# Tail of a fused vision-transformer kernel: weights' parts transposed first, result summed in other banks, one-bank router, fewer filler matmuls, second output transfer issued by ScalarE

## The chip, the cores and the metric

The program runs on one core of a Trainium2 chip. The metric is the device time of one execution in microseconds (us), the median of three executions. The profile shows one further execution. Engines are called PE (TensorE), DVE (VectorE), ACT (ScalarE), POOL (GpSimd) and SP (SyncE), as in the profile.

## What is computed

The reference runs two transformer layers on 8 images of 64 tokens with 64 features: patch embedding and position, attention, a gated feed-forward, a second attention and last a mixture of 8 experts. Only the last part is touched by the change:

```python
def _moe(tokens, router_w, w1, b1, w2, b2):
    logits = tokens @ router_w.T
    probs = softmax(logits)
    rw, re = top_k(probs, 2)
    rw = rw / rw.sum(-1, keepdims=True)
    combine = zeros((N, 8)).at[arange(N)[:, None], re].set(rw)
    out = tokens
    for e in range(8):
        h = gelu(tokens @ w1[e] + b1[e])
        y = h @ w2[e] + b2[e]
        out = out + combine[:, e:e + 1] * y
    return out
...
h = h + _L1_ffn_ref(_layernorm(h), ...)
```

The result adds `h` (the tokens after the second attention), the normalised tokens and the weighted experts.

## The kernel before, in words

512 tokens are kept as two halves of 256: the tile `xC[3]` holds the normalised tokens, features on partitions, with half c=0 on partitions 0 to 63 and half c=1 on 64 to 127. Four slots of 128 tokens are numbered s = 2c + j. Each engine has a program written out by hand, in its own block, and runs it in order; engines meet at semaphores (`wait_ge`, `then_inc`). PSUM has eight banks, `B[0]` to `B[7]`. All float32 matmuls other than transposes are run in two passes, so the trace counts two instructions for each; a transpose by `tr` counts one. `keep_clock(bank, n)` (line 683, instructions at line 687) issues n matmuls of zeros, 128x512 in bfloat16, into a bank that nobody needs at that time; they are called fillers below. Line numbers here are those of the kernel before.

The tail, after the layer norm of the second attention's result:

- PE: the router, four matmuls of 64 rows each, slots of half 0 into `B[2]` and of half 1 into `B[3]` (lines 984 to 988); the first expert layer, eight matmuls for four pairs q of experts, into `B[4]` to `B[7]` (989 to 994); three fillers; after the first two gelus have read `B[4]` and `B[5]` (`s_eg` 2) and after POOL's sum `resT3` (`s_res3`), the opening products of the result `Y = (B[4], B[5])`: the residual by an identity and `Wo1` on `ctxT` (1000 to 1004); two fillers; four transposes of the float32 weights `comb` (1007), four of `comb3`, the same weights as three bfloat16 parts (1012); two fillers; four matmuls with `sel3` that spread the weights of pair q over the hidden rows (1021); three fillers; the products with `b2e` (1026); the second expert layer (1032), which sums all four pairs into `Y`.
- DVE: reads the logits (632), ranks them and forms `lgd`, waits for ACT's tanh `lgt`, forms `comb` and `comb3` (651 to 657), copies the transposed parts to `comb3T` (659), multiplies the gelus by the spread weights, `gs` (668, the last pair in two pieces, one for each j), adds a bias to the second half of the result (670) and copies its transpose to `h4` (672).
- ACT: the gelus `ge` of pairs 0 and 1, the tanh, the gelus of pairs 2 and 3 (426 to 435), a copy `combT` (437), the first half of the result (439) and of its transpose (441).
- SP issues both output transfers (264 and 266), each after its half of `h4` is written.
- POOL has in its queue, in this order: the scaling `WoS` of the first attention's output weights (298), the gather `attr` of edge attributes (309, waits for `s_edge`), two constants, and near the end `resT3` (326).

```python
            for q in range(4):
                for j in range(2):
                    pe.wait_ge(s_gs, q + 1 if q < 3 else 4 + j)
                    for c in range(2):
                        ins = mm(Y[j][rows[c], 0:P], lhsT=w2e[:, q, :], rhs=gs[:, q, c * HALF + j * P:c * HALF + (j + 1) * P], ...
```

Of the kernel before, what the change touches and what calls it, by code (L numbers as in the profile page):

```python
# [6 lines left out]
P = 128  # L7
# [3 lines left out]
D = 64  # L11
# [30 lines left out]
def vit_tower(nc, I, packs, out):  # L42
# [25 lines left out]
    with ctx:  # L68
# [97 lines left out]
        lg = sb("lg", [P, SLOTS, EXPERTS])  # L166
        lgd = sb("lgd", [P, SLOTS, EXPERTS])
# [62 lines left out]
        s_bar = sem("bar_ready")  # L230
# [4 lines left out]
        C3 = B[3][0:3 * EXPERTS, 0:NT // 2].bitcast(bf16)  # L235

# [10 lines left out]
        def _(sp):  # L247
# [22 lines left out]
        def _(pool):  # L270
# [36 lines left out]

            pool.wait_ge(s_edge, 1)
# [20 lines left out]
        def _(act):  # L329
# [96 lines left out]
            for q in range(4):  # L426
                if q == 2:
# [9 lines left out]
            sc.activation(combT[:, :], B[1][0:EXPERTS, :], ACT.Copy).then_inc(s_ct_ev, 1)  # L437
            act.wait_ge(s_fin, 1)
            sc.activation(yT[:, 0, :], B[4][:, 0:P], ACT.Identity, bias=bo_col[:, 0:1]).then_inc(s_yT_a, 1)
            act.wait_ge(s_yR, 1)  # L440
            sc.activation(h4[:, :, :].rearrange("p (c s) d -> p s c d", c=2)[:, 0, :, :],
                          B[6][:, 0:P].rearrange("p (c d) -> p c d", c=2), ACT.Copy).then_inc(s_out_a, 1)

        @block.vector
        def _(dve):
# [186 lines left out]
            link(ve.tensor_copy(lg[:, :, :].rearrange("p (c j) e -> p c (j e)", c=2), psum[:, 2:4, 0:2 * EXPERTS]))  # L632
# [27 lines left out]
            for q in range(4):  # L660
# [4 lines left out]
                         for tile in (gs[:, q, :], ge[:, q, :], (B[2], B[0], B[1], B[3])[q])]  # L665
                for js in (slice(0, 2),) if q < 3 else (slice(0, 1), slice(1, 2)):
# [3 lines left out]
            ve.tensor_scalar(yT[:, 1, :], B[5][:, 0:P], bo_col[:, 0:1], None, ALU.add).then_inc(s_yT_v, 1)  # L670
            dve.wait_ge(s_yR, 2)
            ve.tensor_copy(h4[:, :, :].rearrange("p (c s) d -> p s c d", c=2)[:, 1, :, :],
                           B[7][:, 0:P].rearrange("p (c d) -> p c d", c=2)).then_inc(s_out_v, 1)

        @block.tensor
        def _(pe):
# [330 lines left out]
            for s in range(SLOTS):  # L1007
                ins = tr(B[1][0:EXPERTS, s * P:(s + 1) * P], comb[:, s, :], P)
# [137 lines left out]
```

## Time and profile before

| | us |
|---|---|
| median of three executions | 74.75 (74.56 to 74.87) |
| profiled execution, its own time | 74.51 |
| its span in the profile | 72.7 |
| PE busy in the span | 64.6 (89%) |
| DVE busy | 41.9 (58%) |
| ACT busy | 29.2 (40%) |
| fillers (line 687), all 63 | 19.9 |
| mean granted TensorE clock | 0.992 |

The span runs from the first to the last event of the core; the execution's time contains 1.8 us more around it. A matmul that is pipelined behind another is counted from its own start, so busy times of neighbours overlap: the distance between two starts tells what a matmul takes of PE's time. "PEld" is the weight load that belongs to a matmul. "PEclk" or granted clock is 1.00 at 2.4 GHz and 0.50 at 1.2 GHz.

### The profile page before, as it was taken

The numbers are of one execution on the slowest core, as the hardware profiler recorded it, in microseconds if no ns is written. First come the engines' busy times: TensorE is split into PE (matmuls) and PEld (weight loads), VectorE is DVE, ScalarE is ACT, GpSimd is POOL, SyncE is SP. The second block draws the span as 40 slices with busy tenths as digits, with TensorE's granted clock in tenths as the row PEclk, the third lists the DMA queues.
The fourth block names the chain that finished last, engine by engine and source line by source line (L and its number), as shares of the span: only waits on it lengthen the run. The fifth ranks groups of instructions, "written<-read, shape, count | busy, mean of one in ns | idle before, by whom it ended". The sixth has DMA issues, their size and how long they took to land.

```text
span 72.7 us, 1994 instructions
## 1 busy us (share of the span) xinstructions
PE 64.6 (89%) x843; PEld 39.5 (54%) x843; DVE 41.9 (58%) x108; ACT 29.2 (40%) x63; POOL 13.0 (18%) x29
## 2 busy tenths in 40 slices
PE   3995996999999999989979969799999889999930
PEld 1330554777887585445435645577954285543910
DVE  2590199484799983536642397997540157429430
ACT  0330104404497821296925060488023748530030
POOL 6800094000004920538030000000000030000000
PEclk9999999999999999999999999999999999999996
DMA  0799999900000000000000000000000000000003
GB/s 5 180 394 390 373 224 263 265 16 0 0 9 0 0 9 0 0 0 5 0 0 0 0 0 9 0 9 0 0 9 5 0 0 0 0 0 0 0 0 72
DMA packets 2389, 4.07 MB, mean 56 GB/s; under 512 B 779, under 2 KB 1229, under 8 KB 2381
## 3 DMA queue, kind: packets, MB, share of 16 engines
q1 hardware_dynamic: 1840, 3.55, 16.8%
q10 hardware_dynamic: 509, 0.40, 1.7%
q8 instruction: 6, 0.10, 0.6%
q14 instruction: 2, 0.02, 0.1%
q0 software_dynamic: 32, 0.00, 0.1%
HBM read 3.82 MB, written 0.13 MB: 54 GB/s over the span
## 4 chain that ended last, share of the span: by engine, by line
PE 64%; DVE 13%; DMA 9%; ACT 4%; POOL 3%; issue 3%; DVEq 0%; ACTq 0%; POOLq 0%
PE psum L687 10%; DMA Xt<-in_x_dram 9%; PE psum L681 6%; DVE top L503 3%; POOL WoS L298 3%; PE psum L697 3%; PE psum L893 3%; PE psum L939 3%; PE psum L789 3%; PE psum L740 3%; PE psum L991 3%; PE psum L1032 2%; PE psum L716 2%; DVE E L601 2%; DVE top L599 2%
## 5 line engine op out<-in xcount | busy, mean ns | idle before, releaser
L687 PE MATMUL psum<-warm 128*128 128x512 bf16 x63 | 19.9, 429 | 1.2 <-DVE warm L455 1.2
L687 PEld LDWEIGHTS psum<-warm 128*128 128x128 bf16 x63 | 5.8, 107 | 8.1 <-issue 4.3
L298 POOL TENSOR_TENSOR WoS<-pack_attn,top 128x256 f32<-128x256 f32 x5 | 3.1, 647 | 11.1 <-DVE top L510 11.1
L468 DVE TENSOR_TENSOR onehot<-idb,iota 128x2048 bf16<-128x2048 bf16 x4 | 4.8, 1244 | 0.0
L326 POOL TENSOR_TENSOR resT<-hT,xC 128x256 f32<-128x256 f32 x1 | 0.7, 724 | 20.5 <-DVE xC L630 20.5
L405 ACT ACTIVATE E<-E 128x512 f32<-128x512 f32 x4 | 2.5, 630 | 3.2 <-DVE E L601 3.1
L348 ACT ACTIVATE lv<-psum,eps 128x256 f32<-128x256 f32 x4 | 1.9, 473 | 3.5 <-PE psum L729 0.9
L599 DVE TENSOR_REDUCE top<-psum 128x8 f32<-128x512 f32 x4 | 2.7, 686 | 0.4 <-PE psum L908 0.4
L434 ACT ACTIVATE ge<-psum,pack_moe 128x512 f32<-128x512 f32 x4 | 2.5, 679 | 1.1 <-PE psum L991 1.1
L908 PE MATMUL psum<-kT,qT 9*64 9x64 f32 x128 | 2.1, 231 | 0.9 <-DVE qT L587 0.7
L773 PE MATMUL psum<-top,pack_ident 128*128 128x256 f32 x12 | 2.9, 387 | 0.0
L668 DVE TENSOR_TENSOR gs<-ge,psum 128x512 f32<-128x512 f32 (+1 forms) x5 | 2.5, 577 | 0.5 <-PE psum L1021 0.5
L697 PE MATMUL psum<-Xt,pack_wp 128*64 128x256 f32 x16 | 2.2, 390 | 0.8 <-DMA Xt<-in_x_dram 0.8
L601 DVE TENSOR_TENSOR E<-psum,top 128x512 f32<-128x512 f32 x4 | 2.8, 692 | 0.1
L503 DVE TENSOR_REDUCE top<-psum 128x8 f32<-128x512 f32 x4 | 2.6, 684 | 0.4 <-PE psum L765 0.4
L789 PE MATMUL psum<-WoS,E 128*64 128x64 f32 x64 | 2.7, 227 | 0.1
L630 DVE SCALAR_TENSOR_TENSOR xC<-psum,bo_col,rs 128x256 f32<-128x256 f32 x1 | 0.5, 484 | 4.0 <-ACT rs L350 4.0
L789 PEld LDWEIGHTS psum<-WoS,E 128*64 128x64 f32 x64 | 2.2, 137 | 0.9 <-ACT E L376 0.5
L345 ACT ACTIVATE sq<-psum 128x256 f32<-128x256 f32 x3 | 1.1, 383 | 4.0 <-PE psum L831 1.7
L908 PEld LDWEIGHTS psum<-kT,qT 9*64 9x64 f32 x128 | 1.7, 130 | 1.9 <-ACT qT L400 1.0
L508 DVE TENSOR_REDUCE top<-E 128x8 f32<-128x512 f32 x4 | 2.6, 648 | 0.0
L681 PE MATMUL psum<-pack_ident,E 128*128 128x128 f32 x16 | 2.5, 278 | 0.1
(200 smaller groups left out, 131.7 us busy)
## 6 DMA issues: line engine op xcount, KB each, us to landing
Xt<-in_x_dram SPq DMA_DIRECT2D x1, 1024.0 KB, 6.4
Xt<-in_x_dram SPq DMA_DIRECT2D x1, 512.0 KB, 7.5
pack_both<-in_both_dram SPq DMA_DIRECT2D x2, 240.2 KB, 8.8
pack_moe<-in_moe_dram SPq DMA_DIRECT2D x1, 450.0 KB, 9.8
pack_mid<-in_mid_dram SPq DMA_DIRECT2D x1, 327.5 KB, 10.0
pack_attn<-in_attn_dram SPq DMA_DIRECT2D x1, 288.0 KB, 8.1
pack_expert<-in_expert_dram SPq DMA_DIRECT2D x2, 130.0 KB, 9.3
pack_wp<-in_wp_dram ACTq DMA_DIRECT2D x1, 192.0 KB, 6.0
```

Source lines behind the costliest of these rows:

```text
L298: gp.tensor_tensor(WoS[:, s, 4 * u:4 * u + 4, :].rearrange("p (b n) d -> p b n d", b=2), bc(WoT[:, 2 * u:2 * u + 2, :], 1, 2), bc(top0[:, ...
L468: ve.tensor_tensor(onehot[:, 16 * k:16 * k + 16, :], bc(idb[:, k, :], 1, 16), iota16[:, :, :], ALU.is_equal).then_inc(s_hot, 1)
L503: ve.tensor_reduce(top0[:, 0, s, :].rearrange("p (m q) -> p m q", m=2), S, X, ALU.max, negate=True).then_inc(s_mx0, 1)
L508: ve.tensor_reduce(top0[:, 1, s, :], E0[:, s, :, :], X, ALU.add).then_inc(s_sum0, 1)
L599: ve.tensor_reduce(top, S, X, ALU.max).then_inc(s_mx1, 1)
L601: ve.tensor_tensor(E1[:, s, :, :].rearrange("p (q g) t -> p q g t", g=2), S, bc(top, 3, TOK), ALU.subtract).then_inc(s_sub1, 1)
L681: return nc.tensor.transpose(o, i, ident[0:n, 0:n])
L687: mm(B[bank][:, :], lhsT=warm[:, 0:P], rhs=warm[:, :], start=True, stop=True)
L697: mm(B[0][rows[c], 0:HALF], lhsT=Wp[:, q, :], rhs=Xt[:, c, q, :], start=(q == 0), stop=False)
L773: ins = mm(B[2 * s + m][:, 0:HALF], lhsT=ident, rhs=bc(top0[:, 0, s, 4 * m:4 * m + 4], 2, TOK), start=False, stop=True, skip_group_check=True)
L789: ins = mm(B[2 * s][rows[b], 0:D], lhsT=E0[:, s, i, :], rhs=WoS[:, s, i, :], start=(q == 0), stop=(q == 3))
L908: ins = mm(B[4 * c + hh][b * D:(b + 1) * D, col:col + TOK], lhsT=qT1[rows_, g, tok:tok + TOK], rhs=kT1[rows_, g, tok:tok + TOK], start=Tru ...
```

## The change

It changes seven things in the tail.

1. Router: a new tile `rwB`, [128, 16], holds the router's weights twice, as a block diagonal, zeros elsewhere. POOL fills it (a memset and two copies of 64x8), placed in its queue after `WoS` and ahead of the gather; it waits there for the load of the experts' weights. The router is then two matmuls over all 128 rows, both into `B[2]`, in place of four over 64 rows, and DVE reads the logits from that bank alone.
2. `Y` becomes `(B[0], B[1])`. Its opening products wait only for `s_res3` and follow the first expert layer at once.
3. Fillers: ten in this stretch (3, 2, 2, 3) become one, between the opening products and the transposes.
4. The transposes of `comb3` come first, those of `comb` (now into `B[2]`) behind them; PE waits once, for `s_comb` 5.
5. The spread weights of pair q go to `B[4 + q]`, the banks of the experts' hidden values, so PE waits for gelus 0 and 1 ahead of pair 0, and for gelus 2 and 3 ahead of pair 2. The wait for `combT` moves from ahead of pair 2 to ahead of the `b2e` products.
6. The result's halves are transposed into `B[2]` and `B[3]`.
7. ACT, not SP, issues the transfer of the second half, after waiting for DVE's `s_out_v`.

```diff
+            pool.wait_ge(in_expert, 32)
+            gp.memset(rwB[:, :], 0.0).then_inc(s_rwb, 1)
+            pool.wait_ge(s_rwb, 1)
+            for c in range(2):
+                half = slice(c * D, (c + 1) * D)
+                gp.tensor_copy(rwB[half, c * EXPERTS:(c + 1) * EXPERTS], rwT[half, :]).then_inc(s_rwb, 1)
+            pool.wait_ge(s_rwb, 3)
             pool.wait_ge(s_edge, 1)
...
+            act.wait_ge(s_out_v, 1)
+            act.dma_start(out_v[1], h4_v[:, 1, :, :]).then_inc(out_done, 16)
...
-            pe.wait_ge(in_expert, 32)
+            pe.wait_ge(s_rwb, 3)
             pe.wait_ge(s_x, 4)
-            for s in range(SLOTS):
-                c, j = s // 2, s % 2
-                ins = mm(B[2 + c][:, j * EXPERTS:(j + 1) * EXPERTS], lhsT=xC[3][rows[c], j * P:(j + 1) * P], rhs=rwT[rows[c], :],
+            for j in range(2):
+                ins = mm(B[2][:, 2 * j * EXPERTS:2 * (j + 1) * EXPERTS], lhsT=xC[3][:, j * P:(j + 1) * P], rhs=rwB[:, :],
                          start=True, stop=True)
...
-            Y = (B[4], B[5])
+            Y = (B[0], B[1])
             blocks = [slice(j * P, (j + 1) * P) for j in range(2)]
-            keep_clock(0, 3)
-            pe.wait_ge(s_eg, 2)
+
             pe.wait_ge(s_res3, 1)
...
-            keep_clock(0, 2)
-            pe.wait_ge(s_comb, 1)
-            for s in range(SLOTS):
-                ins = tr(B[1][0:EXPERTS, s * P:(s + 1) * P], comb[:, s, :], P)
-            ins.then_inc(s_ct, 1)
+            keep_clock(3, 1)
+
             pe.wait_ge(s_comb, 5)
             pe.wait_ge(const_moe, 2)
-            for s in range(SLOTS):
-                ins = nc.tensor.transpose(C3[:, s * P:(s + 1) * P], comb3[:, s, :, :], ident_h[:, :])
+            for j in range(2):
+                for c in range(2):
+                    ins = nc.tensor.transpose(C3[:, c * HALF + j * P:c * HALF + (j + 1) * P], comb3[:, 2 * j + c, :, :], ident_h[:, :])
             ins.then_inc(s_c3, 1)
-            keep_clock(2, 2)
+            for j in range(2):
+                for c in range(2):
+                    ins = tr(B[2][0:EXPERTS, c * HALF + j * P:c * HALF + (j + 1) * P], comb[:, 2 * j + c, :], P)
+            ins.then_inc(s_ct, 1)
             pe.wait_ge(s_c3_ev, 1)
             for q in range(4):
 
-                if q == 2:
-                    pe.wait_ge(s_ct_ev, 1)
-                mm((B[2], B[0], B[1], B[3])[q][:, :], lhsT=sel3[:, q, :], rhs=comb3T[:, :], start=True, stop=True).then_inc(s_cr, 1)
-            pe.wait_ge(s_eg, 4)
-            keep_clock(6, 3)
+                if q % 2 == 0:
+                    pe.wait_ge(s_eg, q + 2)
+                mm(B[4 + q][:, :], lhsT=sel3[:, q, :], rhs=comb3T[:, :], start=True, stop=True).then_inc(s_cr, 1)
+            pe.wait_ge(s_ct_ev, 1)
```

How it moves instructions. In these rows a name is the tile written, then `<-` and the tiles read; `warm` is the fillers' operand, `sel` is `sel3`, `comb` with 24x128 is `comb3`.

PE's program from behind the first expert layer to the first spread weights, before:

```order
L687 MATMUL psum<-warm 128x512 x3
L1001 MATMUL psum<-resT,pack_ident 128x128 [waits residual3_ready,expert_gelu]
L1003 MATMUL psum<-ctxT,pack_mid 64x128 x2
L1001 MATMUL psum<-resT,pack_ident 128x128
L1003 MATMUL psum<-ctxT,pack_mid 64x128 x2
L687 MATMUL psum<-warm 128x512 x2
L681 MATMUL psum<-pack_ident,comb 8x128 [waits comb_ready]
L681 MATMUL psum<-pack_ident,comb 8x128 x3
L1013 MATMUL psum<-ident_h,comb 24x128 [waits const_moe,comb_ready]
L1013 MATMUL psum<-ident_h,comb 24x128 x3
L687 MATMUL psum<-warm 128x512 x2
L1021 MATMUL psum<-comb3T,sel 128x512 [waits comb3T_ready]
```

The same place in the changed program, where lines 1006 and 1008 are the opening products, 1016 the transposes of `comb3` and 687 those of `comb`:

```order
L1006 MATMUL psum<-resT,pack_ident 128x128 [waits residual3_ready]
L1008 MATMUL psum<-ctxT,pack_mid 64x128 x2
L1006 MATMUL psum<-resT,pack_ident 128x128
L1008 MATMUL psum<-ctxT,pack_mid 64x128 x2
L693 MATMUL psum<-warm 128x512
L1016 MATMUL psum<-ident_h,comb 24x128 [waits const_moe,comb_ready]
L1016 MATMUL psum<-ident_h,comb 24x128 x3
L687 MATMUL psum<-pack_ident,comb 8x128 x4
L1027 MATMUL psum<-comb3T,sel 128x512 [waits expert_gelu,comb3T_ready]
```

Seven fillers became one, the transposes of the parts stand ahead of those of `comb`, and the opening products no longer wait for a gelu.

PE's program from the second spread weights to the second expert layer, before:

```order
L1021 MATMUL psum<-comb3T,sel 128x512
L1021 MATMUL psum<-comb3T,sel 128x512 [waits combT_ready]
L1021 MATMUL psum<-comb3T,sel 128x512
L687 MATMUL psum<-warm 128x512 [waits expert_gelu]
L687 MATMUL psum<-warm 128x512 x2
L1026 MATMUL psum<-combT,pack_moe 64x128 x4
L1032 MATMUL psum<-gs,pack_moe 64x128 [waits expert_scaled]
```

The same place in the changed program:

```order
L1027 MATMUL psum<-comb3T,sel 128x512
L1027 MATMUL psum<-comb3T,sel 128x512 [waits expert_gelu]
L1027 MATMUL psum<-comb3T,sel 128x512
L1031 MATMUL psum<-combT,pack_moe 64x128 [waits combT_ready]
L1031 MATMUL psum<-combT,pack_moe 64x128 x3
L1037 MATMUL psum<-gs,pack_moe 64x128 [waits expert_scaled]
```

The three fillers are gone and the wait for `combT` stands behind all four matmuls.

POOL's program from the scaling of the first attention's weights, before:

```order
L298 TENSOR_TENSOR WoS<-pack_attn,top 128x256 [waits rinv_ready,const_l1]
L298 TENSOR_TENSOR WoS<-pack_attn,top 128x256
L298 TENSOR_TENSOR WoS<-pack_attn,top 128x256 [waits rinv_ready] x3
L309 DMA attr<-in_L_attn_edge_attr_dram,edge_u 64x3 [waits edge_ready]
L312 TENSOR_SCALAR gate_bar<-pack_mid 128x64 [waits in_mid]
```

and in the changed program:

```order
L297 TENSOR_TENSOR WoS<-pack_attn,top 128x256 [waits rinv_ready,const_l1]
L297 TENSOR_TENSOR WoS<-pack_attn,top 128x256
L297 TENSOR_TENSOR WoS<-pack_attn,top 128x256 [waits rinv_ready] x3
L308 MEMSET rwB 128x16 [waits in_expert]
L312 COPY rwB<-pack_expert 64x8 [waits router_ready]
L312 COPY rwB<-pack_expert 64x8
L315 DMA attr<-in_L_attn_edge_attr_dram,edge_u 64x3 [waits edge_ready,router_ready]
L318 TENSOR_SCALAR gate_bar<-pack_mid 128x64 [waits in_mid]
```

Three small instructions stand between the scaling and the gather.

## Rows read from the trace of the kernel before

**Rows 1.** By stretch: length, busy PE, PEld, DVE, ACT, POOL, granted clock, DMA share, GB/s.
```profile
15.96:23.35 7.39, 7.36 (x161) 6.20 (x162) 5.80 (x12) 4.62 (x13) 0.47 (x1) 1.00 0.01 2
49.84:53.37 3.53, 3.53 (x77) 3.08 (x75) 2.13 (x7) 1.09 (x2) 0.00 (x0) 1.00 0.02 5
```

**Rows 2.** Timeline of PE in the tail: start us, us, engine, line, operation, count.
```profile
58.50 0.62 PE L986 MATMUL psum<-pack_expert,xC 64*128 64x8 f32 x8 [0.70 <-DVE xC L630]
58.94 2.01 PE L991 MATMUL psum<-xC,pack_expert 64*128 64x256 f32 x16
...
60.89 0.82 PE L687 MATMUL psum<-warm 128*128 128x512 bf16 x3
61.54 0.45 PE L1001 MATMUL psum<-resT,pack_ident 128*128 128x128 f32 x2
61.92 0.44 PE L1003 MATMUL psum<-ctxT,pack_mid 64*64 64x128 f32 x4
...
63.08 0.60 PE L687 MATMUL psum<-warm 128*128 128x512 bf16 x2
63.52 0.60 PE L681 MATMUL psum<-pack_ident,comb 128*8 128x128 f32 x4
64.05 0.39 PE L1013 MATMUL psum<-ident_h,comb 128*24 128x128 bf16 x4
64.38 0.61 PE L687 MATMUL psum<-warm 128*128 128x512 bf16 x2
64.95 1.03 PE L1021 MATMUL psum<-comb3T,sel 24*128 24x512 bf16 x4
65.91 0.82 PE L687 MATMUL psum<-warm 128*128 128x512 bf16 x3
66.66 0.65 PE L1026 MATMUL psum<-combT,pack_moe 8*64 8x128 f32 x8
67.25 1.97 PE L1032 MATMUL psum<-gs,pack_moe 128*64 128x128 f32 x32
```

**Rows 3.** Timeline of ACT and DVE in the tail.
```profile
61.57 1.25 ACT L434 ACTIVATE ge<-psum,pack_moe 128x512 f32<-128x512 f32 x2
62.43 0.19 DVE L657 TENSOR_TENSOR comb<-part,comb 128x32 bf16<-128x32 f32 x1
64.16 0.59 ACT L437 ACTIVATE combT<-psum 8x512 f32<-8x512 f32 x1 [1.33 <-PE psum L681]
64.48 0.41 DVE L659 COPY comb3T<-psum 24x512 bf16<-24x512 bf16 x1 [1.86 <-PE psum L1013]
65.44 2.55 DVE L668 TENSOR_TENSOR gs<-ge,psum 128x512 f32<-128x512 f32 x5 [0.55 <-PE psum L1021]
```

**Rows 4.** Timeline: DVE's last copy and the issue of its transfer.
```profile
70.03 0.29 DVE L672 COPY h<-psum 128x128 f32<-128x128 f32 x1 [0.42 <-PE psum L681]
...
70.58 0.47 SPq L266 DMA_DIRECT2D out_dram<-h  x1
```

**Rows 5.** Timeline: full-row float32 weights elsewhere, early fillers, an early issue by ACT.
```profile
1.17 5.30 PE L687 MATMUL psum<-warm 128*128 128x512 bf16 x12 [1.17 <-DVE warm L455]
1.61 0.93 ACTq L333 DMA_DIRECT2D pack_pos<-in_pos_dram  x1
47.10 0.66 PE L681 MATMUL psum<-pack_ident,E 128*128 128x128 f32 x4
47.59 0.59 PE L687 MATMUL psum<-warm 128*128 128x512 bf16 x2
```

**Rows 6.** POOL's timeline, and the page's DMA traffic (GB/s) in 40 slices.
```profile
23.45 2.51 POOL L298 TENSOR_TENSOR WoS<-pack_attn,top 128x256 f32<-128x256 f32 x4
29.83 1.08 POOL L309 DMA_INDIRECT attr<-in_L_attn_edge_attr_dram,edge_u  x1 [3.87 <-DVEq L542]
...
58.44 0.72 POOL L326 TENSOR_TENSOR resT<-hT,xC 128x256 f32<-128x256 f32 x1 [20.53 <-DVE xC L630]
...
GB/s 5 180 394 390 373 224 263 265 16 0 0 9 0 0 9 0 0 0 5 0 0 0 0 0 9 0 9 0 0 9 5 0 0 0 0 0 0 0 0 72
```

More of the change, by code:

```diff
@@ L166, in vit_tower @@
         lg = sb("lg", [P, SLOTS, EXPERTS])
+        rwB = sb("rwB", [P, 2 * EXPERTS])
         lgd = sb("lgd", [P, SLOTS, EXPERTS])
@@ L235, in vit_tower @@
         C3 = B[3][0:3 * EXPERTS, 0:NT // 2].bitcast(bf16)
+        out_v = out.rearrange("(c s b) t d -> s (b t) c d", c=2, s=2)
+        h4_v = h4[:, :, :].rearrange("p (c s) d -> p s c d", c=2)
         block = ctx.enter_context(nc.Block())
@@ L436, in _ @@
             act.wait_ge(s_ct, 1)
-            sc.activation(combT[:, :], B[1][0:EXPERTS, :], ACT.Copy).then_inc(s_ct_ev, 1)
+            sc.activation(combT[:, :], B[2][0:EXPERTS, :], ACT.Copy).then_inc(s_ct_ev, 1)
             act.wait_ge(s_fin, 1)
-            sc.activation(yT[:, 0, :], B[4][:, 0:P], ACT.Identity, bias=bo_col[:, 0:1]).then_inc(s_yT_a, 1)
+            sc.activation(yT[:, 0, :], B[0][:, 0:P], ACT.Identity, bias=bo_col[:, 0:1]).then_inc(s_yT_a, 1)
             act.wait_ge(s_yR, 1)
-            sc.activation(h4[:, :, :].rearrange("p (c s) d -> p s c d", c=2)[:, 0, :, :],
-                          B[6][:, 0:P].rearrange("p (c d) -> p c d", c=2), ACT.Copy).then_inc(s_out_a, 1)
+            sc.activation(h4_v[:, 0, :, :], B[2][:, 0:P].rearrange("p (c d) -> p c d", c=2), ACT.Copy).then_inc(s_out_a, 1)
+            act.wait_ge(s_out_v, 1)
+            act.dma_start(out_v[1], h4_v[:, 1, :, :]).then_inc(out_done, 16)
         @block.vector
@@ L631, in _ @@
             dve.wait_ge(s_lg, 1)
-            link(ve.tensor_copy(lg[:, :, :].rearrange("p (c j) e -> p c (j e)", c=2), psum[:, 2:4, 0:2 * EXPERTS]))
+            link(ve.tensor_copy(lg[:, :, :].rearrange("p s e -> p (s e)"), B[2][:, 0:SLOTS * EXPERTS]))
             dve.wait_ge(in_moe, 16)
@@ L664, in _ @@
                 parts = [tile.rearrange("p (c s t) -> p c s t", c=2, s=2)
-                         for tile in (gs[:, q, :], ge[:, q, :], (B[2], B[0], B[1], B[3])[q])]
+                         for tile in (gs[:, q, :], ge[:, q, :], B[4 + q])]
                 for js in (slice(0, 2),) if q < 3 else (slice(0, 1), slice(1, 2)):
@@ L669, in _ @@
             dve.wait_ge(s_fin, 2)
-            ve.tensor_scalar(yT[:, 1, :], B[5][:, 0:P], bo_col[:, 0:1], None, ALU.add).then_inc(s_yT_v, 1)
+            ve.tensor_scalar(yT[:, 1, :], B[1][:, 0:P], bo_col[:, 0:1], None, ALU.add).then_inc(s_yT_v, 1)
             dve.wait_ge(s_yR, 2)
-            ve.tensor_copy(h4[:, :, :].rearrange("p (c s) d -> p s c d", c=2)[:, 1, :, :],
-                           B[7][:, 0:P].rearrange("p (c d) -> p c d", c=2)).then_inc(s_out_v, 1)
+            ve.tensor_copy(h4_v[:, 1, :, :], B[3][:, 0:P].rearrange("p (c d) -> p c d", c=2)).then_inc(s_out_v, 1)
         @block.tensor
@@ L1036, in _ @@
             pe.wait_ge(s_yT_a, 1)
-            tr(B[6][:, 0:P], yT[:, 0, :], P).then_inc(s_yR, 1)
+            tr(B[2][:, 0:P], yT[:, 0, :], P).then_inc(s_yR, 1)
             pe.wait_ge(s_yT_v, 1)
-            tr(B[7][:, 0:P], yT[:, 1, :], P).then_inc(s_yR, 1)
+            tr(B[3][:, 0:P], yT[:, 1, :], P).then_inc(s_yR, 1)
 _OUTS = [((8, 64, 64), 'float32')]
```

7 lines of the change are left out of this document (2 added, 5 removed).

## The prediction

> **What bounds the kernel now.** I read the chain of waits first: from 58.50 us on it is PE alone, with no wait for another engine, until the last sum; after that ACT, PE and DVE take turns and the transfer ends the span. So I read PE's timeline of the tail next [rows 2] and asked of each group whether PE was doing needed work or bridging a wait. It bridges: ten of its matmuls are fillers, at 60.89 (3), 63.08 (2), 64.38 (2) and 65.91 (3). Then I read DVE and ACT beside it [rows 3]. The last part of the weights is ready at 62.43 + 0.19 = 62.62, yet DVE waits 1.86 us for PE's transposes, because PE is at its opening products, two fillers and the transposes of `comb` first. DVE's products `gs` end at 65.44 + 2.55 = 67.99, and PE goes on to sum for another 1.2 us. PE's program order bounds the tail, fillers included. Last I read the end of the span [rows 4] and the granted clock by stretch [rows 1].
>
> **The change, part by part.** I take distances between starts, since they are what a matmul takes of PE. Everything counts from 58.50, when `xC[3]` is ready; nothing before it moves (POOL's new work is costed last).
>
> Router. Before: eight passes, 58.50 to 58.94, 0.44 [rows 2]. Now four passes over all 128 rows with 16 columns moving. No row of before shows that form. Nearest are float32 weights of 128x128: the opening product takes (61.92 − 61.54)/2 = 0.19 a pass with 128 columns moving [rows 2], the transposes (47.59 − 47.10)/4 = 0.12 [rows 5]. So four passes lie between 4 × 0.055 = 0.22, the pace of the old form (a gain of 0.22), and 4 × 0.19 = 0.76 (a loss of 0.32). I take 0.13 each, 0.52, since with few columns moving the load is what remains and the transposes' row is the nearest to that: a **loss of 0.08**. It delays the logits and the first expert layer alike, hence the weights and the gelus too.
> The Trainium skill speaks otherwise here (TensorE: Matmul & The Clock Gate, section LDWEIGHTS): a load's time goes by its columns, not its rows, so half as many loads of 128 columns would cost half. By that the router would gain 0.22 and the sum below would be 0.30 larger. The two rows above, 0.055 a pass over 64 rows and 0.12 to 0.19 over 128, speak against it.
>
> First expert layer: 58.94 to 60.89, 1.95, unchanged; it now ends at 60.97.
>
> Opening products: 61.54 to 63.08, 1.54, unchanged. The three fillers ahead (0.65) go, and with other banks the wait for gelus 0 and 1 goes too. `resT3`, which they do wait for, is ready at 58.44 + 0.72 = 59.16 [rows 6]. They end at 60.97 + 1.54 = 62.51, and the one filler that remains ((61.54 − 60.89)/3 = 0.22) at 62.73.
>
> Transposes. They need the last part of the weights, 62.62 + 0.08 = 62.70, so PE waits next to nothing; I start them at 62.75. The four of `comb3` take 64.38 − 64.05 = 0.33 and DVE's copy began 0.43 after the first of them [rows 2, 3]: it runs from 63.18 to 63.59. The four of `comb` take 0.53 and now lie beside that copy, ending at 63.61.
>
> Spread weights: from 63.65 (0.06 after the copy, as before), 0.96 long. The gelus they wait for end about 61.53 and at 61.57 + 1.25 + 0.08 = 62.90 [rows 3], both earlier. The new place of the wait for `combT` costs nothing: ACT's 0.59 starts at about 63.65, ends at 64.25, and PE asks for it at 64.61. That cover is 0.36; without it `b2e` would slip by what is missing.
>
> `b2e` from 64.61, 0.59 long; second expert layer from 65.20, before 67.25 [rows 2]. That is **2.05 earlier**, and by parts: fillers 0.65 + 0.22 (one of the two at 63.08) + 0.57 + 0.75 = 2.19, less 0.08 router, less about 0.06 of now exposed waits.
>
> Does DVE hold it up? The first `gs` begins 0.49 after the spread weights, at 64.14, and the five end 2.55 later at 66.69. PE, unhindered, would end its 32 passes 1.97 + 65.20 = 67.2; the last four need DVE's last piece and would take until about 66.69 + 0.4 = 67.1. PE still ends last, by 0.1: the two are nearly level, so this part can gain no more from PE alone.
>
> End of the span: everything behind the last sum comes 2.05 earlier, by the same steps. Before, DVE's copy ended at 70.03 + 0.29 = 70.32, but SP issued the second transfer at 70.58, because it was still issuing the first [rows 4]. ACT is idle, so it issues some 0.05 after the copy: 0.21 gained. Against that, an issue by ACT took 0.93 early in the program, beside SP's issues, where SP's took 0.47 here [rows 4, 5]. So the ends are a gain of 0.3 and a loss of 0.25; I take **0.20 gained**, since here only two transfers are in flight.
>
> POOL: three small instructions between `WoS`, done at 25.96, and the gather at 29.83, for which POOL idles 3.87 [rows 6]. Even at the 0.63 of a `WoS` product each they fit with 1.9 to spare: 0. The experts' weights have long landed: traffic ends in the ninth of 40 slices of 1.82 us, by 16.4 us [rows 6].
>
> Sum: 2.05 + 0.20 = 2.25. The profiled execution took 74.51, so it would take 72.26; the median of the three is 0.24 above it, so I predict 74.75 − 2.25 = **72.5 us**. A difference under 0.5% (0.37 us) is about what a measurement of this kernel cannot tell from none.
>
> **The rivals.**
>
> A. *The clock falls (slower).* After the one filler at 62.5 PE has none to the end, with eight transposes, small matmuls and waits. If it dropped to 1.2 GHz, every pass would take up to twice as long. A price at such a pace is in the trace: the twelve fillers at the start are (5.30 − 0.43)/11 = 0.44 apart, against 0.22 in the tail [rows 5, 2] (the granted-clock column says 1.00 there too, so I use the row for its size alone). From the spread weights on, 0.96 + 0.59 + 1.97 + 0.38 (the two last transposes at 0.19) = 3.90 would be added: 72.5 + 3.9 = 76.4. It decides from 2.25 us of added PE time, so only when the clock falls by about the start of the second expert layer; a fall behind that leaves the change faster. For it: ten fillers stood where one will. Against it: two stretches without a filler, 7.4 us of small matmuls and 3.5 us with eight transposes and tiny products among them, both at 1.00 [rows 1], and PE here has no gap over 0.1 us until the last sum. I give it 9%: 7% slower, 2% near no change.
> The Trainium skill has a rule for this rival (TensorE: Matmul & The Clock Gate, part 4): transposes do not count as busy for the clock in the same way. By it the clock would be nearer to falling in the stretch of eight transposes; the row from 49.84 to 53.37, with as many, shows no such thing.
>
> B. *The logits' chain takes over.* PE reaches the transposes with 0.03 us in hand, so whatever delays DVE's or ACT's chain shows at once: with the router at its dear end, 0.32 lost in place of 0.08, both chains shift and the gain is 2.0; if in addition DVE's `gs` runs slower against PE, now that both end together, 0.3 more is lost: 74.75 − 1.7 = 73.05. For it: DVE and PE nearly level. Against: nothing they share is used more than before. 12%.
>
> C. *ACT's issue is as dear as the dear row*, or the two transfers land no sooner side by side: 2.05 − 0.25 = 1.8 gained, 72.95. 10%.
>
> D. *The router costs half*, and ACT issues at 0.38: 2.25 + 0.30 + 0.1 = 2.65, 72.1. 12%.
>
> The forecast itself, 2.0 to 2.5 gained, has 57%.
>
> **How the numbers follow.** The forecast and B, C, D (91%) are faster by 1.7 to 2.65, and span 72.1 to 73.05. Adding 0.3 for the executions' own spread and for two bounds falling together on either side gives a range of 71.8 to 73.4; left out are rival A and the corners. Of A's 9%, 7 are slower and 2 within 0.5%; another 1% within 0.5% is kept for losses that I don't see. So: faster 0.90, same 0.03, slower 0.07.
>
> **What the profile after would show.** Four router passes about 0.13 apart. No filler behind the first expert layer; opening products from about 61.0; `comb3T` at 63.2 and DVE's wait ahead of it under 1 us in place of 1.86. `gs` from 64.1. Second expert layer ending near 67.2, and its four last passes close behind DVE's last piece. An output issue on ACT at some 68.3, overlapping SP's. The gather still at 29.8 and a granted clock of 1.00 to the last transpose. I am wrong if the clock column falls ahead of 67 us, if PE shows waits of over 0.2 us for DVE at the transposes, or if the first expert layer starts later than 59.2.

## The result, and the profile after

| | before | after |
|---|---|---|
| median, us | 74.66 | 72.52 |
| lowest to highest of four, us | 74.56 to 74.87 | 72.24 to 72.68 |
| profiled execution: time, span, us | 74.51, 72.7 | 72.43, 70.6 |
| PE busy, us | 64.6 | 62.7 |
| fillers, all of the program | 63, 19.9 us | 54, 17.4 us |

The ratio is 0.9705, with an interval of 0.9665 to 0.9745: **2.1 us faster**, where 72.5 us was predicted (71.8 to 73.4). In some executions of most kernels here TensorE's granted clock falls for a while; the ratios, and the times where not all are listed, are of executions in which it did not.

One thing that the list of the change's parts left out: with the new router the logits come out as slot 2j + c in place of 2c + j, and the loops over `comb` and `comb3` are renumbered to match. It moves no instruction.

The first part of the changed kernel's page (busy us of each engine, share of the span, instructions):

```profile
PE 62.7 (89%) x830; PEld 38.7 (55%) x830; DVE 41.8 (59%) x108; ACT 29.2 (41%) x63; POOL 13.5 (19%) x32
```

PE's share of the span is 89% before and after. The share says nothing about the gain, since a filler counts as busy as a product does; that nine fillers are gone is seen in the last row of the table. The timeline of the tail shows the rest (the columns of [rows 2 to 4]):

```profile
58.57 0.59 PE L991 MATMUL psum<-rwB,xC 128*128 128x16 f32 x4 [0.70 <-DVE xC L637]
59.09 2.00 PE L997 MATMUL psum<-xC,pack_expert 64*128 64x256 f32 x16
59.20 0.19 DVE L639 COPY lg<-psum 128x32 f32<-128x32 f32 x1 [0.77 <-PE psum L991]
...
61.02 0.49 PE L1006 MATMUL psum<-resT,pack_ident 128*128 128x128 f32 x2
...
62.47 0.19 DVE L664 TENSOR_TENSOR comb<-part,comb 128x32 bf16<-128x32 f32 x1
...
62.59 0.39 PE L693 MATMUL psum<-warm 128*128 128x512 bf16 x1
...
62.91 0.39 PE L1016 MATMUL psum<-ident_h,comb 128*24 128x128 bf16 x4
...
63.34 0.41 DVE L666 COPY comb3T<-psum 24x512 bf16<-24x512 bf16 x1 [0.67 <-PE psum L1016]
...
63.81 1.03 PE L1027 MATMUL psum<-comb3T,sel 24*128 24x512 bf16 x4
63.87 0.59 ACT L443 ACTIVATE combT<-psum 8x512 f32<-8x512 f32 x1 [1.00 <-PE psum L687]
64.30 2.54 DVE L675 TENSOR_TENSOR gs<-ge,psum 128x512 f32<-128x512 f32 x5 [0.55 <-PE psum L1027]
...
64.77 0.65 PE L1031 MATMUL psum<-combT,pack_moe 8*64 8x128 f32 x8
...
65.35 1.98 PE L1037 MATMUL psum<-gs,pack_moe 128*64 128x128 f32 x32
67.16 0.37 ACT L445 ACTIVATE yT<-psum,bo_col 128x128 f32<-128x128 f32 x1 [2.70 <-PE psum L1037]
...
68.16 0.29 DVE L679 COPY h<-psum 128x128 f32<-128x128 f32 x1 [0.42 <-PE psum L687]
68.25 0.41 SPq L265 DMA_DIRECT2D out_dram<-h  x1
68.48 0.41 ACTq L449 DMA_DIRECT2D out_dram<-h  x1
```

The router starts at 58.57, so nothing ahead of it gained: all of the difference lies in the tail. I read it as distances from the router's first pass, since these don't shift when the start of the program does. They repeat well: to the second expert layer it is 6.78 in this profile and in that of `e_sp_issues`, whose tail has the same instructions up to there. To the second expert layer it is 67.25 − 58.50 = 8.75 before [rows 2] and 65.35 − 58.57 = 6.78 after, 1.97 less. To the issue of the second output it is 70.58 − 58.50 = 12.08 [rows 2, 4] and 68.48 − 58.57 = 9.91, 2.17 less. The span falls by 2.1 and not by 2.17, because the router starts 0.07 later. DVE's wait for the transposes of `comb3` is 0.67 in place of 1.86 [rows 3].

The granted clock in the stretch with the eight transposes (length, busy us of PE, PEld, DVE, ACT and POOL with their counts, clock, DMA share, GB/s):

```profile
62.00:64.00 2.00, 2.00 (x16) 0.97 (x16) 1.01 (x6) 1.00 (x3) 0.00 (x0) 1.00 0.00 0
```

It is full speed, 2.4 GHz, here and in every other stretch from 55 us to the last output's issue.

### The profile page after: what moved, and what is told of

It reads as the page before. It is cut to its first block, busy times and chain, and to the rows that moved or that the text cites. A ratio compares the mean times of both kernels' runs of the same rounds, so it can differ in the third digit from the quotient of the medians.

```text
span 70.6 us, 1972 instructions
## 1 busy us (share of the span) xinstructions
PE 62.7 (89%) x830; PEld 38.7 (55%) x830; DVE 41.8 (59%) x108; ACT 29.2 (41%) x63; POOL 13.5 (19%) x32
## 4 chain that ended last, share of the span: by engine, by line
PE 66%; DMA 9%; DVE 7%; ACT 6%; issue 3%; POOL 3%; DVEq 0%; ACTq 0%; POOLq 0%
DMA Xt<-in_x_dram 9%; PE psum L693 9%; PE psum L687 6%; POOL WoS L297 3%; PE psum L703 3%; PE psum L914 3%; PE psum L899 3%; PE psum L945 3%; PE psum L795 3%; PE psum L997 3%; PE psum L746 3%; ACT E L377 2%; PE psum L1037 2%; PE psum L722 2%; PE psum L859 2%
## 5 line engine op out<-in xcount | busy, mean ns | idle before, releaser
L693 PE MATMUL psum<-warm 128*128 128x512 bf16 x54 | 17.4, 437 | 1.2 <-DVE warm L462 1.2
L693 PEld LDWEIGHTS psum<-warm 128*128 128x128 bf16 x54 | 5.3, 108 | 7.0 <-issue 3.6
```

The lines of the kernel that those rows point to most:

```text
L693: mm(B[bank][:, :], lhsT=warm[:, 0:P], rhs=warm[:, :], start=True, stop=True)
```

## The experiments

The theory: PE's order bounded the tail, so each part is worth what it takes off PE's path, and the parts add up (fillers 0.65 + 0.22 + 0.57 + 0.75; order of transposes and banks to let them go; ACT's issue 0.20; router −0.08). The rivals: DVE's chain takes over when PE is freed; the clock needs the fillers; the gain comes from the banks or the issue and the fillers were free. Distances are from the router's first pass, and "to w2e" is to the second expert layer's first.

**Fillers alone, on the kernel before** (`e_before_nofill`).

```diff
-            keep_clock(0, 3)
             pe.wait_ge(s_eg, 2)
...
-            keep_clock(0, 2)
+            keep_clock(0, 1)
...
-            keep_clock(2, 2)
             pe.wait_ge(s_c3_ev, 1)
...
-            keep_clock(6, 3)
```

> The kernel before with nine of the ten fillers of the tail taken out and nothing else (the one left stands behind the opening products). Theory: the fillers are only part of the gain; the opening products still wait for the gelus 0 and 1 (until about 61.45 us), the float32 transposes still stand ahead of the parts', so the second expert layer starts near 66.2 instead of 67.25: about 1.0 us gained on before, 73.65 us. Rival: the fillers are all of it: 2.2 us gained, 72.5 us.

Measured: the one execution without a fall of the clock took 73.75, where before took 74.79 to 75.1 on that chip; three more, 74.93 to 75.59, had a lower mean clock, in the profiled one early in the program and not in the tail. The distances in that tail:

```profile
60.36 0.62 PE L986 MATMUL psum<-pack_expert,xC 64*128 64x8 f32 x8 [0.70 <-DVE xC L630]
...
63.36 0.49 PE L1000 MATMUL psum<-resT,pack_ident 128*128 128x128 f32 x2 [0.55 <-ACT ge L434]
...
65.69 0.39 PE L1012 MATMUL psum<-ident_h,comb 128*24 128x128 bf16 x4
...
66.59 1.03 PE L1019 MATMUL psum<-comb3T,sel 24*128 24x512 bf16 x4 [0.51 <-DVE comb3T L659]
...
68.14 1.99 PE L1029 MATMUL psum<-gs,pack_moe 128*64 128x128 f32 x32
```

To w2e 7.78, which is 0.97 less than before: not quite half of the change. The first three fillers give nothing, because PE then waits for gelus 0 and 1 in their place, as the bracket behind L1000 shows: to the opening products it is 3.00, against 61.54 − 58.50 = 3.04 before [rows 2]. Nor do the two at the spread weights: from the transposes of `comb3` to the spread weights it is 66.59 − 65.69 = 0.90, as before (64.95 − 64.05 [rows 2]), since PE waits for DVE's copy there (the bracket behind L1019). What comes back is one filler (about 0.2) and the three ahead of `b2e` (0.75). A filler is a cost only where no wait stands behind it that would last as long.

**The wait for the gelus, put back into the change** (`e2_wait_gelu`): what moving the sums to other banks is worth.

```diff
+            pe.wait_ge(s_eg, 2)
             pe.wait_ge(s_res3, 1)
```

> The changed kernel with the wait for gelus 0 and 1 put back ahead of the opening products (as if Y still lay in their banks). Theory: the products start at 61.65 instead of 61.02, and all behind is 0.6 us later: second expert layer 7.4 us after the router's first pass instead of 6.78, 73.1 us. Rival: the wait is hidden by that for the weights (62.7 us), under 0.1 us.

Measured: 73.00 in one execution. The opening products start 61.56 − 58.48 = 3.08 after the router instead of 2.45, and w2e 7.41 instead of 6.78: **0.63**.

```profile
58.48 0.59 PE L991 MATMUL psum<-rwB,xC 128*128 128x16 f32 x4 [0.70 <-DVE xC L637]
...
61.56 0.49 PE L1007 MATMUL psum<-resT,pack_ident 128*128 128x128 f32 x2 [0.56 <-ACT ge L440]
...
63.88 0.41 DVE L666 COPY comb3T<-psum 24x512 bf16<-24x512 bf16 x1 [1.30 <-PE psum L1017]
...
65.89 1.98 PE L1038 MATMUL psum<-gs,pack_moe 128*64 128x128 f32 x32
```

DVE's wait grows by the same 0.63, from 0.67 to 1.30. So the first three fillers and this wait are one cost of 0.65 that could only go together, and the other banks are what lets both go.

**The transposes in their old order** (`e_order_old`).

```diff
+            pe.wait_ge(s_comb, 1)
+            for j in range(2):
+                for c in range(2):
+                    ins = tr(B[2][0:EXPERTS, c * HALF + j * P:c * HALF + (j + 1) * P], comb[:, 2 * j + c, :], P)
+            ins.then_inc(s_ct, 1)
             pe.wait_ge(s_comb, 5)
...
-            for j in range(2):
-                for c in range(2):
-                    ins = tr(B[2][0:EXPERTS, c * HALF + j * P:c * HALF + (j + 1) * P], comb[:, 2 * j + c, :], P)
-            ins.then_inc(s_ct, 1)
```

> The changed kernel with the transposes of comb ahead of those of its parts, as before. Theory: the parts' transposes start 0.53 later, less what PE waited there: comb3T, the spread weights and everything behind 0.4 to 0.5 us later than in the changed kernel, 72.95 us. Rival: the order is worth nothing, since PE must do both anyway: 72.5 us.

Measured: 73.22 and 73.51, and 74.58 and 76.58 with a lower mean clock; the ratio of the first two to before, 0.9884 (0.976 to 1.0008), says little. In the profile, at full clock, it is to w2e 66.14 − 58.92 = 7.22, **0.44** more than the change.

```profile
58.92 0.59 PE L991 MATMUL psum<-rwB,xC 128*128 128x16 f32 x4 [0.70 <-DVE xC L637]
...
62.94 0.39 PE L693 MATMUL psum<-warm 128*128 128x512 bf16 x1
...
63.16 0.60 PE L687 MATMUL psum<-pack_ident,comb 128*8 128x128 f32 x4
63.69 0.39 PE L1021 MATMUL psum<-ident_h,comb 128*24 128x128 bf16 x4
...
66.14 1.99 PE L1038 MATMUL psum<-gs,pack_moe 128*64 128x128 f32 x32
```

It is the 0.53 of the four transposes of `comb`, less 0.10: the filler holds PE for 0.22 here (62.94 to 63.16) and for 0.32 in the change (62.59 to 62.91).

**Three fillers back, ahead of `b2e`** (`e_fill_back`). They had looked as if they bridged the wait for the gelus.

```diff
+            keep_clock(3, 3)
             pe.wait_ge(s_ct_ev, 1)
```

> The changed kernel with three fillers put back between the spread weights and the b2e products. Theory: PE, not DVE, ends the sum, by about 0.1 us, so three fillers of 0.22 cost 0.6 to 0.65 us: 73.15 us. Rival: DVE's products bound this part, PE has slack there and the fillers cost under 0.2 us.

Measured: 73.19, 73.01 and 73.66, ratio 0.9792 (0.9739 to 0.9845); a fourth took 76.37 at a mean clock of 0.954.

```profile
58.58 0.59 PE L991 MATMUL psum<-rwB,xC 128*128 128x16 f32 x4 [0.70 <-DVE xC L637]
...
64.31 2.54 DVE L675 TENSOR_TENSOR gs<-ge,psum 128x512 f32<-128x512 f32 x5 [0.55 <-PE psum L1027]
64.78 0.82 PE L693 MATMUL psum<-warm 128*128 128x512 bf16 x3
65.53 0.65 PE L1032 MATMUL psum<-combT,pack_moe 8*64 8x128 f32 x8
66.11 1.97 PE L1038 MATMUL psum<-gs,pack_moe 128*64 128x128 f32 x32
```

To w2e 7.53, **0.75** more, and the block takes 65.53 − 64.78 = 0.75, as before (66.66 − 65.91 [rows 2]). I had expected 0.6 to 0.65, three times 0.22, and the rival had DVE's `gs` cover it. They do not: `gs` starts where it did, 5.73 after the router, and PE is late by the whole block. These three were pure cost.

**SP issues both outputs** (`e_sp_issues`).

```diff
-            act.wait_ge(s_out_v, 1)
-            act.dma_start(out_v[1], h4_v[:, 1, :, :]).then_inc(out_done, 16)
...
+            sp.wait_ge(s_out_v, 1)
+            sp.dma_start(out_v[1], h4_v[:, 1, :, :]).then_inc(out_done, 16)
```

> The changed kernel with SP issuing both output transfers. Theory: the second issue starts 0.2 us later and the span ends 0.2 later: 72.7 us. Rival: two queues at once land no earlier: 72.5 us.

Measured: 72.63, 73.02 and 73.05, ratio 0.9721 (0.9669 to 0.9773), and 74.8 and 74.92 with a lower mean clock. The profiled execution, 74.8, lost clock early in the program; its end, at full clock:

```profile
70.33 0.29 DVE L679 COPY h<-psum 128x128 f32<-128x128 f32 x1 [0.42 <-PE psum L687]
70.42 0.41 SPq L265 DMA_DIRECT2D out_dram<-h  x1
70.87 0.47 SPq L267 DMA_DIRECT2D out_dram<-h  x1
```

From DVE's copy's end, 70.62, to the second issue it is 0.25; in the change 68.48 − 68.45 = 0.03. From the router to the second issue it is 70.87 − 60.74 = 10.13 against 9.91, so ACT's issue is worth **0.22**, and the transfer takes 1.7 from issue to landing either way. The ratio alone, whose interval overlaps that of the change, would not have shown it.

**The old router** (`e_router_old`). Four matmuls over 64 rows, two banks; it keeps the filler, and leaves out the renumbering, so that the slots' weights are exchanged in this kernel; the times of the instructions don't depend on it.

```diff
-            pe.wait_ge(s_rwb, 3)
             pe.wait_ge(s_x, 4)
-            for j in range(2):
-                ins = mm(B[2][:, 2 * j * EXPERTS:2 * (j + 1) * EXPERTS], lhsT=xC[3][:, j * P:(j + 1) * P], rhs=rwB[:, :],
+            for s in range(SLOTS):
+                c, j = s // 2, s % 2
+                ins = mm(B[2 + c][:, j * EXPERTS:(j + 1) * EXPERTS], lhsT=xC[3][rows[c], j * P:(j + 1) * P], rhs=rwT[rows[c], :],
                          start=True, stop=True)
...
+            pe.wait_ge(s_lgd, 1)
             keep_clock(3, 1)
```

> The changed kernel with the old router: four matmuls of 64 rows into two banks, no work of POOL for it (PE waits for the logits' gap lgd ahead of its one filler, because the filler's bank held logits; lgd is ready 1 us earlier). Theory: eight passes in 0.44 us where the new router takes 0.52, so all behind comes 0.08 earlier. Rival: half as many loads of 128 columns were cheaper, so the old router would take 0.2 us more; or the read of one bank made DVE's chain shorter by itself.

Measured: 73.38 in one execution, later than the change by 0.95, though its tail is shorter: the router starts at 59.55, 0.98 late. 0.58 of that is the first embedding product, which begins at 7.71 instead of 7.13 because its input lands later, and 0.38 is a pause of PE ahead of the router that the last section comes to. Neither is the router's.

```profile
59.55 0.62 PE L984 MATMUL psum<-pack_expert,xC 64*128 64x8 f32 x8 [0.70 <-DVE xC L629]
59.99 2.01 PE L989 MATMUL psum<-xC,pack_expert 64*128 64x256 f32 x16
60.21 0.19 DVE L631 COPY lg<-psum 128x32 f32<-128x32 f32 x1 [0.81 <-PE psum L984]
...
66.27 1.99 PE L1030 MATMUL psum<-gs,pack_moe 128*64 128x128 f32 x32
```

The old router takes 0.44 of PE, the new 0.52. But DVE copies the logits 0.66 after the first pass here and 0.63 after it in the change. To w2e it is 6.72 against 6.78, so with the filler in place the new router costs 0.06.

**No filler at all in the tail** (`e_no_filler`, and `e2_no_filler` again on another chip).

```diff
-            keep_clock(3, 1)
-
             pe.wait_ge(s_comb, 5)
```

> The changed kernel without its last filler in the tail. Theory: the weights' parts are ready at 62.66 us and the filler holds PE until 62.9, so the parts' transposes start 0.15 earlier and the rest with them: 72.35 us, clock at 1.00 to the end. Rival: the filler keeps the clock up; without it the clock falls to 0.50 before the end and the time rises by 1 us or more.

> The changed kernel without its last filler, once more, beside the kernel with the old router. Theory: 72.2 us as before, ratio 0.964 to before; in the profile the parts' transposes start 4.15 us after the router's first pass.

Measured: medians 72.17 and 72.11 of all six executions each, ratios 0.9642 (0.9604 to 0.9679) and 0.9662 (0.9629 to 0.9694). One of the twelve, 74.17, had a lower mean clock. Of `e_no_filler` the profile:

```profile
58.58 0.59 PE L991 MATMUL psum<-rwB,xC 128*128 128x16 f32 x4 [0.70 <-DVE xC L637]
...
62.48 0.19 DVE L664 TENSOR_TENSOR comb<-part,comb 128x32 bf16<-128x32 f32 x1
62.73 0.39 PE L1014 MATMUL psum<-ident_h,comb 128*24 128x128 bf16 x4
...
65.17 1.99 PE L1035 MATMUL psum<-gs,pack_moe 128*64 128x128 f32 x32
```

The transposes now start 0.06 after DVE's last part (62.67), and w2e 6.59 after the router: **0.19** less. In the second chip's profile it is 64.76 − 58.16 = 6.60. Here DVE's and ACT's chain for the weights is what PE waits for, and taking more off PE ahead of the transposes can't help.

**No filler and the old router** (`e_best`, the four matmuls with the row halves alternating and the slots exchanged as in `e_router_old`; then `e2_router_old`, in the order of before and with DVE's copy of the logits sorting the slots).

```diff
+            link(ve.tensor_copy(lg[:, :, :].rearrange("p (j c) e -> p c j e", c=2), psum[:, 2:4, 0:2 * EXPERTS].rearrange("p c (j e) -> p c j e", j=2)))
```

> No last filler, and the router as four matmuls of 64 rows again, ordered so that neighbours use different row halves. Theory: 0.15 from the filler and 0.08 from the router, a little more if loads for different row halves overlap: 72.2 us. Rival: DVE's chain of the logits bounds the start of the transposes and only the filler's 0.15 is seen: 72.35 us.

> The same without the last filler, and with four router matmuls of 64 rows into two banks, no router work on POOL, the logits copied in the changed kernel's slot order. Theory: the router's first pass to the parts' transposes takes 4.15 us too, since the logits leave either router at the same time (0.63 to 0.65 us after its first pass) and bound the transposes; any difference of the whole time, up to 0.6 us, lies at 46 us, where PE waits for nothing the profile names in the middle of the score matmuls. Rival: the router itself makes the difference, and it shows between the router and the transposes.

Measured: `e_best` 72.53 to 72.65 in three executions and 73.99 to 74.14 in three with a mean clock of 0.973 to 0.976, ratio of the first three 0.9701 (0.9655 to 0.9746); `e2_router_old` 71.96 to 72.72 in six of seven, 0.9678 (0.9636 to 0.972). Neither beats `e2_no_filler`. In both the transposes of `comb3` start 4.15 and 4.16 after the router's first pass (64.61 − 60.46, 62.77 − 58.61), and in the two without a filler and with the new router 4.15 and 4.16 too (62.73 − 58.58, 62.32 − 58.16). Without the filler the **router is worth nothing**, in either direction. Alternating the halves takes 60.90 − 60.46 = 0.44, as without.

`e2_router_old` showed rival A as well. Six of its seven executions kept the clock; in the profiled one, 73.90, it fell in the tail (columns as in the table of stretches above):

```profile
65.00:66.00 1.00, 1.00 (x12) 0.72 (x10) 1.00 (x3) 0.00 (x0) 0.00 (x0) 0.53 0.00 0
66.00:67.00 1.00, 1.00 (x14) 1.00 (x12) 0.71 (x3) 0.00 (x0) 0.00 (x0) 0.50 0.00 0
67.00:68.00 1.00, 1.00 (x14) 1.00 (x12) 0.00 (x0) 0.00 (x0) 0.00 (x0) 0.50 0.00 0
68.00:69.00 1.00, 0.80 (x10) 0.56 (x6) 0.15 (x1) 0.37 (x1) 0.00 (x0) 0.77 0.00 0
```

The clock was at 1.00 until 65.0, at 0.50 from 65.1 to 68.4 and at 1.00 again from 68.5 on. The second expert layer, which began at 65.32, lasted 3.48 in place of 1.99. From the router to the second output's issue it was 69.95 − 58.61 = 11.34, against 68.31 − 58.58 = 9.73 in `e_no_filler`: +1.6.

**The five fillers ahead of the router** (`e_best_no5`, then `e2_no_five` with the rest of the change whole). They lie in PE's wait for `xC[3]`, so by PE's path they are free; are they of use?

```diff
-            keep_clock(2, 5)
             pe.wait_ge(s_rwb, 3)
```

> As e_best, and the five fillers behind the variance's matmul are gone too, so PE is idle for 1.7 us before the router and has no filler for the rest of the program. Theory: those five lay wholly in a wait, so with the clock at 1.00 the time is that of e_best, 72.2 us. Rival A of the prediction: with a longer idle stretch the granted clock falls to 0.50 in the tail and the time rises, by up to 4 us.

> The changed kernel without the five fillers behind the variance's matmul (PE then idles 1.8 us ahead of the router); the one behind the opening products stays. Theory: with the clock up the time is the changed kernel's, 72.5 us; in some executions the clock falls to 0.50 at the router and the first expert layer takes 3.6 us instead of 1.9: 74.1 us. Rival: only the kernel without any later filler loses the clock, here none does.

Measured, all executions: `e_best_no5` 73.76, 72.23, 79.41, 73.98; `e2_no_five` 74.05, 74.09, 82.75, 79.56, 72.24, 77.67, with a mean clock of 0.976, 0.976, 0.840, 0.890, 1.000 and 0.896. The profiled one of 74.05:

```profile
58.00:59.00 1.00, 0.45 (x4) 0.48 (x4) 0.41 (x1) 1.00 (x1) 0.52 (x1) 1.00 0.00 0
59.00:60.00 1.00, 1.00 (x8) 0.88 (x9) 0.75 (x3) 0.09 (x1) 0.21 (x1) 0.79 0.00 0
60.00:61.00 1.00, 1.00 (x8) 0.78 (x6) 0.90 (x3) 0.20 (x1) 0.00 (x0) 0.50 0.00 0
```

```profile
58.55 0.59 PE L990 MATMUL psum<-rwB,xC 128*128 128x16 f32 x4 [1.78 <-DVE xC L637]
59.07 3.34 PE L996 MATMUL psum<-xC,pack_expert 64*128 64x256 f32 x16
```

PE idles 1.78 ahead of the router, and about a microsecond after it starts again the clock goes to 0.50 (1.2 GHz), from 59.6 to 62.9, which covers most of the first expert layer, which lasts 62.34 − 59.07 = 3.27 in place of 1.93. Where the clock stays up, the kernel takes 72.24, no less than with the fillers. In `e_best_no5` the profile shows the same fall, 0.4 after the router's start (0.50 from 59.0 to 62.3). So these five cost nothing on PE's path, and without them eight of ten executions took 1.5 us more or worse; in the six of these that were not profiled, where it fell was not seen. Executions with a lower mean clock exist with the five in place too, and the count has to be read against them: on the same two chips, 6 of 30 executions of the other variants of the changed kernel (three of them of `e_best`) and 2 of 22 of the kernel before. `e_best_no5` alone, with 3 of 4 against 3 of 6 of `e_best`, would show little; `e2_no_five`, with 5 of 6 against 1 of 14 of the others on its chip, shows that the five matter.

## Why the prediction was right, point by point

The parts, as predicted and as the runs measured them, in distances on PE's path to w2e:

| part | predicted | measured | by |
|---|---|---|---|
| three fillers and the wait for gelus behind them | 0.65 | 0.63 | `e2_wait_gelu` |
| one filler of the two behind the opening products | 0.22 | 0.18 | `e_before_nofill` |
| transposes of `comb` into the copy's time, two fillers there | 0.57 | 0.44 | `e_order_old` |
| three fillers ahead of `b2e` | 0.75 | 0.75 | `e_fill_back` |
| router | −0.08 | −0.06 | `e_router_old` |
| waits that the fillers had covered | −0.06 | | |
| sum to w2e | 2.05 | 1.94 by the parts above, 1.97 by the profiles | change |
| ACT's issue | 0.20 | 0.20 to 0.22 | change, `e_sp_issues` |
| router to second issue | 2.25 | 2.17 | change |

The 0.18 is the distance from the opening products to the next transposes, 65.16 − 63.36 = 1.80 in `e_before_nofill` against 63.52 − 61.54 = 1.98 before [rows 2].

The mechanism was right: PE's order bounded the tail, and the gain is what left PE's path. That 72.5 was met to 0.02 is in part luck: the medians differ by 2.14 and not by 2.25, and the median of before came out at 74.66, not at the 74.75 that the gain was taken from. One label in the sum was wrong. It lists 0.57 among the fillers, as the price of the two at 64.38, but in its own working that stretch gains by the transposes of `comb` (0.53), which move beside the copy, and `e_before_nofill` shows that the two fillers alone give nothing: 0.90 from the transposes of `comb3` to the spread weights with them and without.

**Router**: 0.52 was predicted and 0.52 measured, 0.13 a pass. The nearest row, the transposes over 128 rows, had 0.12 [rows 5]; no row of before had this form, so the hit rests on choosing that row over the bounds of 0.055 and 0.19. The Trainium skill's rule (TensorE: Matmul & The Clock Gate, LDWEIGHTS), that a load goes by its columns and not by its rows, would have made it 0.22, and this trace does not agree. One step of mine was wrong: "it delays the logits and the first expert layer alike". PE's path is 0.08 longer, but the logits leave no later, 0.63 after the first pass against 0.66 (58.50 to 59.16 before). Before, DVE's copy began 0.22 after PE had gone on to the expert layer (59.16 against 58.94), now 0.11 (59.20 against 59.09): what DVE waits for is the last result, and that is not PE's next start. Why it is sooner in this form was not tested. So the weights were ready 62.66 − 58.57 = 4.09 after the router, not 4.20. In the change the filler hid that; without the filler the router has no effect on the transposes' start.

**Opening products and filler**: from 61.02 (60.97 predicted). The filler that remains was priced at 0.22, the step inside a block of fillers; it holds PE for 0.32 ahead of the transposes of `comb3`. By the prediction's sum it cost next to nothing, since it ended at 62.73 and the weights were ready at 62.70. It was the bound: 0.19 by `e_no_filler`. This is the largest miss on PE's path, and with the start of the router 0.07 later it accounts for transposes at 62.91 instead of 62.75.

**From the transposes on** every distance came as forecast: copy 0.43 after the first transpose, spread weights 0.47 after the copy's start, `b2e` 0.96 behind them, w2e 0.58 behind that. ACT's cover for `combT` was 64.77 − 64.46 = 0.31 (0.36 predicted).

**DVE and PE level** at the end: `gs` ends at 66.84, and ACT's read of the first sum starts at 67.16. From w2e's start to that read it is 1.81. In `e_fill_back`, where `gs` ends at 66.85, a full microsecond ahead of the read at 67.91, it is 1.80. DVE did not hold PE up by more than 0.01, so rival B's second half did not occur. Its first half, the logits' chain taking over, is what `e_no_filler` found, 0.2 further on than the change goes.

**End**: ACT issued 0.03 after DVE's copy; its issue took 0.41, not the 0.93 of the early row, so rival C did not occur. Both outputs landed 1.7 us after their issue.

**POOL**: the memset and two copies took from 25.81 to 26.44 and POOL then idled 3.89. The cost of 0 was right, but not the reason: the idle time of 3.87 was taken for slack, and the gather moved by 0.5 all the same (last section). PE reads its result at 34.0, as before (34.1).

**Rival A**, the clock, did not come true in the four executions of the change. It is real, once in seven executions of `e2_router_old`. I had it at 3.9 us and deciding from 2.25, with the clock low from the spread weights to the end. That fall cost 1.6: it came at 65.0, in the middle of the `b2e` products, and the clock was back at 68.5, ahead of the last two transposes (0.54, as in the others). So hit, that kernel took 73.90, still under the 74.67 of the kernel before; the step of this rival that does not fit is that a fall lasts to the end. On the rule of the Trainium skill about transposes and the clock (TensorE: Matmul & The Clock Gate, part 4): the stretch with eight of them kept 1.00 in the change, and in the one fall in the tail the clock went down 2.2 us behind the first of them (62.77). The runs neither bear the rule out nor exclude it.

**The best version found** is the change without its last filler, 71.85 to 72.43 in 11 of 12 executions on two chips; the twelfth took 74.17 at a mean clock of 0.976, and where it fell was not seen. Its intervals overlap that of the change, so the times alone don't show it to be better; the profiles put it 0.19 ahead.

## What to carry to other kernels

Price a filler by what stands behind it on its engine. If that is a wait which would last as long anyway, the filler is free and removing it gives nothing, as the first three here until the banks were changed; if it is work that is ready, it costs its full length, as the three ahead of `b2e` (0.75). Before removing a free one, see how long the engine would idle: the five ahead of the router cost nothing, and without them the clock fell far more often.

When one engine's order is shortened, look for the second chain that comes level, and stop there: a router that is 0.08 dearer on PE did not matter once DVE's chain of weights was the later one.

## What the runs showed of the hardware

- **The clock can fall after a short idle stretch.** With 1.78 us of idle PE ahead of the router the mean clock was down in eight of ten executions of two kernels; with 0.70 of idle time there (the five fillers in place) no profile shows a fall at that place. Idle time is not the whole of it: in `e2_router_old` the clock fell at 65.0 with PE busy all the time from 63 on.
- **Half clock, and how long it lasted.** All six profiles with a fall show 0.50 for 3.3 to 3.4 us and then 1.00 again (in `e_best_no5` from 59.0 to 62.3). Inside it float32 passes took twice as long: there the first expert layer began at 59.09 and lasted 3.56, that is 3.26 at half clock, worth 1.63 at full, and 0.30 behind it, together the 1.93 of the others. Executions with a mean clock of 0.971 to 0.977 took some 1.5 to 1.9 us longer than those without a fall; those of 77 to 83 us, at 0.84 to 0.896, were not profiled.
- **Falls at the start.** In the profiled executions of `e_before_nofill`, `e_sp_issues` and `e_best` the clock fell at 7.3 to 8.3 us, behind PE's wait for its first inputs, and was back by 11.8. That wait was 1.97 to 2.10 in these three and 0.58 to 1.84 in the eleven profiles whose clock held there. The router started at 60.36 to 60.74, where it is 58.16 to 59.55 in the others. The code there is the same in all kernels here, so such an execution says nothing of an edit in the tail.
- **A pause of PE that no edit made.** Behind the 52nd of the 64 score products around 46 us PE idles, with "issue" as the only reason, for a time that differs between kernels whose code there is the same:

```profile
46.61 0.36 PE L908 MATMUL psum<-kT,qT 9*64 9x64 f32 x12 [0.27 <-issue]
```

```profile
46.68 0.36 PE L914 MATMUL psum<-kT,qT 9*64 9x64 f32 x12 [0.45 <-issue]
```

  The first is of the kernel before, the second of the change; it was 0.29 in `e_no_filler`, 0.55 in `e2_router_old`, 0.61 in `e_best` and 0.83 in `e_router_old`. In `e_fill_back` and `e_before_nofill` there is none, and `e2_no_filler`, the same kernel as `e_no_filler`, had 0.20. The cause was not found. Up to some 0.2 the pause costs nothing, and what is longer is lost: from the first of these score products to the router it is 58.58 − 45.66 = 12.92 in `e_fill_back`, 58.50 − 45.53 = 12.97 before, 58.57 − 45.42 = 13.15 in the change and 59.55 − 46.01 = 13.54 in `e_router_old`. This is why the change's router starts 0.07 later though its first embedding product begins 0.11 earlier (7.13 against 7.24). It is as large as the effects looked for, and a reason to read them as distances in the tail.
- **A router pass over 128 rows** takes 0.13 with 16 columns moving, one over 64 rows 0.055 with 8, and alternating the row halves between passes changes nothing (0.44 for eight passes either way).
- **POOL's gather** started at 30.33 in place of 29.83 [rows 6], with its index ready at the same time (DVE's `edge_u`, which starts at 29.23 and 29.34) and POOL idle for 3.89 ahead of it. In all fourteen profiles it starts 3.86 to 3.90 behind the end of POOL's last instruction, while it starts 0.95 behind its index in those with the three new instructions and 0.35 in those without. So it followed POOL's own queue and not its index; why it takes 3.9 was not tested. Nothing waited for it.
